# Hi and lo parts of six stationary operands, laid side by side element by element

## The chip, the cores and the metric

One core of one Trainium2 chip runs the kernel. The metric is the device time of one execution in microseconds (us), as the median of several runs.

## What is computed

The input `x` is (8, 1024, 256): 8 batches, 1024 tokens, 256 channels. Each token is normalised (layer norm without weights) to `xn`. Two blocks read `xn`, and the output is `x` plus both:

```python
# attention: 8 heads of 128, one shared key/value head, causal
q = xn @ Wq + bq                 # (T, 8, 128), plus positions
k, v = split(xn @ Wkv + bkv)     # (T, 128) each, k plus positions
out = softmax(mask(q @ k.T / sqrt(128))) @ v @ Wo
# channel mix
xr = mu_r * xn + (1 - mu_r) * xn_prev      # xn_prev: the token before
xk = mu_k * xn + (1 - mu_k) * xn_prev
ffn = sigmoid(xr @ W_r.T) * (relu(xk @ W_k.T) ** 2 @ W_v.T)
```

All is float32.

## The kernel before

**High and low parts.** TensorE is fed with tiles of type `float32r` (`R` in the code), which keep fewer bits than float32. So every operand is kept as two tiles: index 0 the rounded value (a copy on ScalarE), index 1 what is left (a subtraction on VectorE or GpSimd). A product then takes three passes of matmuls into the same accumulator: high by high, high by low, low by high (`PASSES`; `product` at L1036 does this for all but two kinds of work). `matmul(out, a, m)` loads `a`, 128 columns, into the array (an LDWEIGHTS, engine PEld in the profile) and streams `m` past it. Here `a` is called the standing or stationary operand, `m` the moving one. Each matmul has its own load.

**Order of work.** A batch has 1024 tokens in 8 tiles of 128 and 4 chunks of 256. A step `s` (64 per batch) takes 16 queries of all 8 heads, which makes 128 rows, against the keys up to them. The scores of a step have 16 to 1024 columns; from tile 4 on they are made in two halves. The steps are pipelined by fixed lags: scores (L1036, `pS<-kt,qt`), mask and minimum on VectorE, exponential on ScalarE, scaling on GpSimd, then the turn of the probabilities, for 40 of the 64 steps by TensorE (L1139) and for 24 by VectorE and a round trip through DRAM, and last the product with `v` (L1173, `pO<-pt,v`). Between these stand fillers, in an order written out by hand in `TURNS` and `WO_AT`:

- `Q`, four per chunk, 12 matmuls of 256 columns each: standing `wq`, moving `xt`.
- `KV`, one per chunk, 12 matmuls: standing `wkv`, moving `xt`.
- `FK`, 12 matmuls: standing `wk`, moving `mh`.
- `FR`, 12 matmuls: standing `mh`, moving `wr`.
- `FV`, 12 matmuls: standing `kh`, moving `wv`.
- `WO`, one per tile of 128 tokens, 24 matmuls (L1123): standing `ot`, moving `wo`.

In the scores `qt` stands and `kt` moves. In the product with `v`, `v` stands and `pt` moves; where the block on the diagonal is packed, one matmul with `vs` (L1181) takes the place of its three.

**Who writes the six operands of the change.** The weights are written once, at the start (`weight_hi`, `weight_lo`). `qt`: ScalarE at L661, GpSimd at L527. `ot`: ScalarE at L759, VectorE at L994. `kh`: ScalarE at L705, GpSimd at L590. The last three are written in each batch, in chunks or pairs of steps; `qt` and `ot` are scattered in runs of 16 elements already.

**Where the tiles lie.** `sb(...)` gives each tile the next free bytes of every partition, in the order of the code. All sizes down to `kh` and `ot` are multiples of 1024 bytes, so only `gap` shifts what comes after it: `xt`, `mh`, `wv`, `kt`, `pt`, `wo` start at a multiple of 1024, and `wq` to `ot` 64 bytes past one.

Of the kernel before, what the change touches and what calls it, by code (L numbers as in the profile page):

```python
# [4 lines left out]
B, T, E = 8, 1024, 256  # L5
H, D = 8, 128
P = 128
CT = E // P
CHUNK = 256
# [4 lines left out]
SUB = P // H  # L14
# [204 lines left out]
def build(nc, x_d, wq_d, wkv_d, wo_d, wr_d, wk_d, wv_d, bq_d, bkv_d, mu_d, pet_d, out_d, park_d):  # L219
    F, R = mybir.dt.float32, mybir.dt.float32r  # L220
# [5 lines left out]
    with ExitStack() as ctx:  # L226
        def sb(name, shape, dt=F):
            return ctx.enter_context(nc.sbuf_tensor(name, shape, dt))
# [11 lines left out]
        kt = [sb(f"kt{i}", [P, T], R) for i in range(2)]  # L240
        pt = [sb(f"pt{i}", [P, 2, NT, 2 * P], R) for i in range(2)]
        wo = [sb(f"wo{i}", [P, H, E], R) for i in range(2)]
        gap = sb("gap", [P, 16])
        wq = [sb(f"wq{i}", [P, CT, H * D], R) for i in range(2)]
        wk = [sb(f"wk{i}", [P, CT, E], R) for i in range(2)]
        wkv = [sb(f"wkv{i}", [P, CT, 2 * D], R) for i in range(2)]
        wr = [sb(f"wr{i}", [P, CT, E], R) for i in range(2)]
        kh = [sb(f"kh{i}", [P, CT, CHUNK], R) for i in range(2)]
        qt = [sb(f"qt{i}", [P, 2, CHUNK // SUB, H, SUB], R) for i in range(2)]
        v = [sb(f"v{i}", [P, NT, D], R) for i in range(2)]  # L250
        vs = sb("vs", [P, TPC, D], R)
        ot = [sb(f"ot{i}", [P, H, P], R) for i in range(2)]
        bq = sb("bq", [P, H])
        mu = sb("mu", [P, 4])
        omu = sb("omu", [P, 4])
# [1021 lines left out]
```

## Time and profile before

| | |
|---|---|
| median of 3 runs | 1517.11 us (1516.37 to 1522.73) |
| span of the profiled execution, first to last instruction | 1512.0 us |
| span of that execution beside the median | 5.1 us less |
| PE busy | 1484.7 us, 98% |
| DVE busy | 1262.6 us, 84% |
| POOL busy | 1153.7 us, 76% |
| ACT busy | 1052.6 us, 70% |
| matmuls, and as many weight loads | 11724 |

Busy time of PE is the union of its matmuls; a matmul's record runs from its start until its last column has left the array, so two that follow each other overlap. To see how fast the stream is, take the duration of a group of equal matmuls, subtract one matmul's duration and divide by their number less one: that is the distance from start to start. DVE is VectorE, ACT is ScalarE, POOL is GpSimd, SP is the engine that issues DMAs.

### The profile page before, as it was taken

Reading aid. Unit: us, or ns where it says so; the run is one execution under the profiler, and the core shown is the slowest. Engines: PE = TensorE matmul, PEld = TensorE weight load, DVE = VectorE, ACT = ScalarE, POOL = GpSimd, SP = SyncE. Lnnn points to the kernel's source line nnn. Section 1 sums busy time; section 2 is a strip of 40 time slices with the busy share of each in tenths; the row PEclk is TensorE's granted clock in tenths of the full one; section 3 lists DMA queues with packets and bytes.
Section 4 is the critical chain, followed back from the end, with each engine's and each line's share of the span. In section 5 each row is a group of like instructions: output and inputs, shape, how many; then the busy total and the mean of one; then the engine's idle time right before and its main releaser. Section 6 shows DMA issues by size and latency. Waiting matters only on the chain.

```text
span 1512.0 us, 36188 instructions
## 1 busy us (share of the span) xinstructions
PE 1484.7 (98%) x11724; PEld 1448.2 (96%) x11724; DVE 1262.6 (84%) x3424; ACT 1052.6 (70%) x2531; POOL 1153.7 (76%) x1665
## 2 busy tenths in 40 slices
PE   7999999999999999999999999999999999999998
PEld 6999999999999999999999999999999999999998
DVE  7988869888698896988879888788887988879875
ACT  5777667776677766767677676767767776777764
POOL 6787777787777787877778777778777787778774
PEclk9999999999999999999999999999999999999999
DMA  4144422444224542344423444134441344413453
GB/s 129 44 126 135 132 87 67 116 141 141 74 69 119 146 137 60 86 120 139 128 58 96 120 137 136 43 100 122 137 139 38 105 130 138 138 29 101 127 153 105
DMA packets 225801, 164.39 MB, mean 109 GB/s; under 512 B 51792, under 2 KB 220880, under 8 KB 225616
## 3 DMA queue, kind: packets, MB, share of 16 engines
q1 hardware_dynamic: 224768, 161.69, 37.1%
q8 instruction: 96, 1.57, 0.4%
q14 instruction: 89, 0.73, 0.2%
q10 hardware_dynamic: 848, 0.40, 0.1%
HBM read 81.27 MB, written 77.59 MB: 105 GB/s over the span
## 4 chain that ended last, share of the span: by engine, by line
PE 75%; DVE 10%; DMA 7%; SPq 3%; issue 3%; ACT 1%; POOL 1%; DVEq 0%; ACTq 0%; POOLq 0%
PE pS L1036 26%; PE pO L1173 21%; PE pG L1036 12%; PE pG L1123 8%; PE pT L1139 7%; DMA park_dram<-Y 5%; SPq L455 3%; DVE X L1015 2%; DVE mix L861 1%; DMA Z<-park_dram 1%; DVE Y L924 1%; DVE pt L940 1%; DVE qtmp L850 1%; PE pS L1123 1%; DVE xn L810 1%
## 5 line engine op out<-in xcount | busy, mean ns | idle before, releaser
L766 ACT ACTIVATE X<-X,bias 128x16 f32<-128x16 f32 (+56 forms) x512 | 376.0, 734 | 156.3 <-DVE bias L1015 154.8
L1036 PE MATMUL pS<-kt,qt 128*128 128x288 f32 (+41 forms) x2304 | 462.2, 329 | 4.1 <-DVE kv L837 2.5
L1173 PE MATMUL pO<-pt,v 128*128 128x256 f32 x3288 | 435.4, 283 | 2.5 <-DVE ot L994 2.4
L1173 PEld LDWEIGHTS pO<-pt,v 128*128 128x128 f32 x3288 | 399.8, 189 | 3.6 <-DVE ot L994 3.4
L575 POOL TENSOR_SCALAR X<-X,rec 128x16 f32<-128x16 f32 (+56 forms) x512 | 373.6, 730 | 26.9 <-DVE rec L914 16.2
L1015 DVE CUSTOM_DVE_ANT_0 X<-pS,mask 128x16 f32<-128x16 f32 (+56 forms) x512 | 353.7, 691 | 40.8 <-PE pS L1036 33.9
L1036 PEld LDWEIGHTS pS<-kt,qt 128*128 128x128 f32 x2304 | 365.2, 189 | 16.8 <-issue 3.7
L542 POOL TENSOR_TENSOR pt<-Z,pt 128x256 fp32r<-128x256 f32 (+5 forms) x192 | 317.7, 1655 | 78.7 <-ACT pt L688 77.8
L527 POOL TENSOR_TENSOR qt<-qtmp,qt 128x256 fp32r<-128x256 f32 x252 | 194.5, 772 | 62.8 <-ACT qt L661 55.2
L940 DVE TENSOR_TENSOR pt<-pT,pt 128x512 fp32r<-128x512 f32 (+3 forms) x440 | 207.7, 493 | 37.9 <-ACT pt L695 37.1
L759 ACT CAST ot<-pO 128x256 fp32r<-128x256 f32 x256 | 95.9, 375 | 173.4 <-PE pO L1173 94.3
L695 ACT CAST pt<-pT 128x512 fp32r<-128x512 f32 (+3 forms) x448 | 189.6, 453 | 11.8 <-PE pT L1139 11.4
L1139 PE MATMUL pT<-ident,X 128*128 128x128 f32 x1248 | 190.1, 274 | 0.8 <-DVE pt L940 0.8
L924 DVE STREAM_TRANSPOSE Y<-X 128x384 f32<-128x384 f32 (+5 forms) x192 | 172.1, 896 | 6.2 <-POOL X L575 3.8
L994 DVE TENSOR_TENSOR ot<-pO,ot 128x256 fp32r<-128x256 f32 x256 | 106.6, 416 | 83.6 <-ACT ot L759 82.1
L1123 PE MATMUL pG<-wo,ot 128*128 128x256 f32 x1344 | 169.7, 282 | 1.3 <-DVE qtmp L850 0.7
L688 ACT CAST pt<-Z 128x384 fp32r<-128x384 f32 (+5 forms) x192 | 148.1, 771 | 31.1 <-DMA Z<-park_dram 30.0
L1123 PEld LDWEIGHTS pG<-wo,ot 128*128 128x128 f32 x1344 | 160.0, 189 | 3.0 <-DVE qtmp L850 2.3
L1139 PEld LDWEIGHTS pT<-ident,X 128*128 128x128 f32 x1248 | 150.6, 141 | 9.9 <-POOL X L575 0.7
L1036 PE MATMUL pG<-xt,wq 128*128 128x256 f32 x1116 | 148.8, 283 | 1.3 <-POOL xt L515 0.8
L1036 PEld LDWEIGHTS pG<-xt,wq 128*128 128x128 f32 x1116 | 141.6, 190 | 4.5 <-DVE xtok L975 2.3
L573 POOL MEMSET X<- 128x16 f32 (+5 forms) x336 | 48.0, 143 | 105.1 <-DVE rec L914 104.5
(118 smaller groups left out, 1943.4 us busy)
## 6 DMA issues: line engine op xcount, KB each, us to landing
park_dram<-Y SPq DMA_DIRECT2D x32, 512.0 KB, 2.6
Z<-park_dram SPq DMA_DIRECT2D x128, 128.0 KB, 3.0
park_dram<-Y SPq DMA_DIRECT2D x32, 448.0 KB, 3.2
Z<-park_dram SPq DMA_DIRECT2D x128, 112.0 KB, 2.7
park_dram<-Y SPq DMA_DIRECT2D x32, 384.0 KB, 2.9
Z<-park_dram SPq DMA_DIRECT2D x128, 96.0 KB, 2.5
park_dram<-Y SPq DMA_DIRECT2D x32, 320.0 KB, 2.9
Z<-park_dram SPq DMA_DIRECT2D x128, 80.0 KB, 2.2
```

What stands on the lines that cost most here:

```text
L527: nc.gpsimd.tensor_tensor(qt[1][:, slot, :, h, :], qtmp[:, p % QTMP, i, :].rearrange("p (t q) -> p t q", q=SUB), qt[0][:, slot, :, h, :].b ...
L542: nc.gpsimd.tensor_tensor(pt_of(1, s)[:, 0:whole, :].rearrange("p k (a c) -> p a k c", a=4), Z[:, k % 2, :, 0:whole, :], pt_of(0, s)[:, 0: ...
L575: nc.gpsimd.tensor_scalar(x_row(s, 0, w), x_row(s, 0, w), rec[:, j:j + 1], 1.0, ALU.mult, ALU.mult).then_inc(normed, 1)
L695: nc.scalar.copy(pt_of(0, s)[:, k:k + nk, :], pT[u % 2][:, 0:nk * P].rearrange("p (k n) -> p k n", n=P)).then_inc(t_hi, 1)
L766: nc.scalar.activation(x_row(s, 0, w), x_row(s, 0, w), ACT.Exp, bias=bias[:, j:j + 1], scale=-1.0, accum_out=total[:, j:j + 1]).then_inc(e ...
L924: nc.vector.transpose(Y[:, k % 2, :, 0:nk, :].rearrange("p a k c -> p k a c"), x_row(s, 0, nk * P).rearrange("p (k a c) -> p k a c", a=4, ...
L940: low = nc.vector.tensor_tensor(pt_of(1, s)[:, k:k + whole, :], pT[u % 2][:, 0:whole * P].rearrange("p (k n) -> p k n", n=P), pt_of(0, s)[ ...
L1015: nc.vector.tensor_tensor_reduce(out=o, in0=scores, in1=m, scale=SCALE, scalar=HUGE, op0=ALU.add, op1=ALU.min, accum_out=bias[:, j:j + 1]) ...
L1036: last = nc.tensor.matmul(out, a[i], m[j], start=start and k == 0, stop=stop and k == n - 1)
L1123: last = nc.tensor.matmul(out[:, 0:E], ot[i][:, h, :], wo[j][:, h, :], start=(i, j, h) == (0, 0, 0), stop=i == 1 and h == H - 1)
L1139: last = nc.tensor.transpose(pT[u % 2][:, i * P:(i + 1) * P], x_row(s, (k + i) * P, (k + i + 1) * P), ident[:, :])
L1173: last = nc.tensor.matmul(pO[:, 0:2 * P], v[i][:, k, :], pt[j][:, pair % 2, k, :], start=n == 0, stop=n == 3 * nk - 1)
```

## The change

The pairs of tiles for `wq`, `wk`, `wkv`, `kh`, `qt` and `ot` become one tile each with a last dimension of 2: element 0 is the high part, element 1 the low one. Views with the old names index that dimension, so that the code that reads and writes them is as before, now with a step of 8 bytes from element to element in place of 4. The tiles also change order: `wqs`, `qts` and `ots` come right after `wo`; a gap of 32 bytes stands ahead of `wks`, another ahead of `wkvs`, a third ahead of `khs`. `wr`, `v` and `vs` come after two of the gaps.

```diff
-        gap = sb("gap", [P, 16])
-        wq = [sb(f"wq{i}", [P, CT, H * D], R) for i in range(2)]
-        wk = [sb(f"wk{i}", [P, CT, E], R) for i in range(2)]
-        wkv = [sb(f"wkv{i}", [P, CT, 2 * D], R) for i in range(2)]
+        wqs = sb("wqs", [P, CT, H * D, 2], R)
+        qts = sb("qts", [P, 2, CHUNK // SUB, H, SUB, 2], R)
+        ots = sb("ots", [P, H, P, 2], R)
+        gap0 = sb("gap0", [P, 8])
+        wks = sb("wks", [P, CT, E, 2], R)
+        gap1 = sb("gap1", [P, 8])
+        wkvs = sb("wkvs", [P, CT, 2 * D, 2], R)
         wr = [sb(f"wr{i}", [P, CT, E], R) for i in range(2)]
-        kh = [sb(f"kh{i}", [P, CT, CHUNK], R) for i in range(2)]
-        qt = [sb(f"qt{i}", [P, 2, CHUNK // SUB, H, SUB], R) for i in range(2)]
         v = [sb(f"v{i}", [P, NT, D], R) for i in range(2)]
         vs = sb("vs", [P, TPC, D], R)
-        ot = [sb(f"ot{i}", [P, H, P], R) for i in range(2)]
+        gap2 = sb("gap2", [P, 8])
+        khs = sb("khs", [P, CT, CHUNK, 2], R)
+        wq, wk, wkv, kh = [[w[:, :, :, i] for i in range(2)] for w in (wqs, wks, wkvs, khs)]
+        qt = [qts[:, :, :, :, :, i] for i in range(2)]
+        ot = [ots[:, :, :, i] for i in range(2)]
```

## Rows read from the trace of the kernel before

**Rows 1.** The page, busy us (share) xinstructions, and granted clock in 40 slices:
```profile
PE 1484.7 (98%) x11724; PEld 1448.2 (96%) x11724; DVE 1262.6 (84%) x3424; ACT 1052.6 (70%) x2531; POOL 1153.7 (76%) x1665
...
PEclk9999999999999999999999999999999999999999
```

**Rows 2.** The page, chain that ended last, by engine:
```profile
PE 75%; DVE 10%; DMA 7%; SPq 3%; issue 3%; ACT 1%; POOL 1%; DVEq 0%; ACTq 0%; POOLq 0%
```

**Rows 3.** Waits of PE, the longest: us in total, times, longest us:
```profile
PE pG L1081 <- DVE xtok L975: 4.1, 8, 0.6
```

**Rows 4.** Busy time of each engine in two stretches of a batch's length:
```profile
core 0: us, PE busy (x) PEld busy (x) DVE busy (x) ACT busy (x) POOL busy (x), PEclk, DMA share, GB/s
100.00:285.00 185.00, 184.07 (x1464) 179.90 (x1463) 155.94 (x426) 130.39 (x316) 143.72 (x208) 1.00 0.39 109
285.00:470.00 185.00, 183.93 (x1460) 179.72 (x1459) 155.81 (x426) 130.02 (x314) 143.03 (x206) 1.00 0.37 107
```

**Rows 5.** Order of time, PE: start us, us, instructions (x so many):
```profile
65.30 0.70 PE L1036 MATMUL pS<-kt,qt 128*128 128x400 f32 x3
...
193.96 1.56 PE L1036 MATMUL pS<-kt,qt 128*128 128x512 f32 x6
...
204.71 0.93 PE L1139 MATMUL pT<-ident,X 128*128 128x128 f32 x7
...
564.25 1.56 PE L1036 MATMUL pS<-kt,qt 128*128 128x512 f32 x6
...
593.71 1.66 PE L1036 MATMUL pS<-wr,mh 128*128 128x256 f32 x12
595.20 1.53 PE L1036 MATMUL pG<-xt,wq 128*128 128x256 f32 x12
...
622.17 2.98 PE L1123 MATMUL pS<-wo,ot 128*128 128x256 f32 x24
...
651.88 0.96 PE L1036 MATMUL pS<-kt,qt 128*128 128x288 f32 x6
...
667.33 3.09 PE L1123 MATMUL pG<-wo,ot 128*128 128x256 f32 x24 [0.26 <-DVE qtmp L850]
...
672.87 1.64 PE L1036 MATMUL pG<-xt,wq 128*128 128x256 f32 x12
```

**Rows 6.** Weight loads: three beside scores of 224 columns, and a mean:
```profile
601.22 0.41 PEld L1036 LDWEIGHTS pS<-kt,qt 128*128 128x128 f32 x3
...
L1036 PEld LDWEIGHTS pS<-kt,qt 128*128 128x128 f32 x2304 | 365.2, 189 | 16.8 <-issue 3.7 <-DVE kt L832 1.5 <-DVE bias L1015 0.6
```

**Rows 7.** Matmuls by form: busy us, mean ns of one:
```profile
L1139 PE MATMUL pT<-ident,X 128*128 128x128 f32 x1248 | 190.1, 274 | 0.8 <-DVE pt L940 0.8
L1123 PE MATMUL pG<-wo,ot 128*128 128x256 f32 x1344 | 169.7, 282 | 1.3 <-DVE qtmp L850 0.7 <-ACT ot L759 0.6
L1036 PE MATMUL pG<-xt,wq 128*128 128x256 f32 x1116 | 148.8, 283 | 1.3 <-POOL xt L515 0.8
...
L1036 PE MATMUL pS<-kt,qt 128*128 128x512 f32 x72 | 19.4, 395 | 0.0
L1036 PE MATMUL pS<-kt,qt 128*128 128x400 f32 x72 | 15.6, 343 | 0.0
L1036 PE MATMUL pS<-kt,qt 128*128 128x288 f32 x72 | 12.2, 295 | 0.0
```

**Rows 8.** Writers on ACT, POOL, DVE by form: busy us, mean ns of one:
```profile
L661 ACT CAST qt<-qtmp 128x512 fp32r<-128x512 f32 x128 | 79.8, 623 | 7.6 <-DVE qtmp L850 7.5
L679 ACT CAST mh<-mix 128x512 fp32r<-128x512 f32 x64 | 39.9, 624 | 24.8 <-DVE mix L861 18.4 <-PE pS L1036 6.3
...
L527 POOL TENSOR_TENSOR qt<-qtmp,qt 128x256 fp32r<-128x256 f32 x252 | 194.5, 772 | 62.8 <-ACT qt L661 55.2 <-DVE rec L914 7.4
L521 POOL TENSOR_TENSOR v<-kv,v 128x256 fp32r<-128x256 f32 x32 | 23.9, 746 | 5.3 <-ACT v L657 5.0
...
L994 DVE TENSOR_TENSOR ot<-pO,ot 128x256 fp32r<-128x256 f32 x256 | 106.6, 416 | 83.6 <-ACT ot L759 82.1
L975 DVE TENSOR_TENSOR xtok<-pG,xtok 128x256 f32<-128x256 f32 x56 | 23.2, 415 | 4.9 <-PE pG L1123 4.4
```

## Prediction

> **What bounds the kernel now.** I read the page's busy shares first, then the chain, TensorE's waits, and last its instructions in order of time. TensorE is busy for 98% of the span at full granted clock, which is the 2.4 GHz level [rows 1]. The chain that ended last is on PE for 75% [rows 2], and what PE waits for longest comes to 4.1 us in all, over 8 waits [rows 3]. Two stretches of 185 us, one batch each, show the same busy time within 0.2 us, with DVE at 84% and POOL at 77% [rows 4]. The kernel is a stream of 11,724 pairs of weight load and matmul, and its time is set by how far apart two matmuls start.
>
> That distance is the number to look at. A group of x matmuls of duration d lasts (x - 1) starts and one d. Means of one: 282 to 283 ns at 256 columns, 295 at 288, 343 at 400, 395 at 512, 274 for a transpose [rows 7]. With them the groups in order of time [rows 5] give:
> - seven transposes, whose standing operand is plain float32: (0.93 - 0.274)/6 = 109.3 ns;
> - twelve of `Q`: (1.53 - 0.283)/11 = 113.4 ns in one place, (1.64 - 0.283)/11 = 123.4 in another, the same code (the second holds a pause of some 80 ns before its second matmul, as the 24 of `WO` also do; without it 117 to 118);
> - 24 of `WO`: with such a pause of 85 ns taken off, (2.98 - 0.282 - 0.085)/23 = 113.6 on bank pS and (3.09 - 0.282 - 0.085)/23 = 118.4 on pG;
> - twelve of `FR` (standing `mh`, moving `wr`): (1.66 - 0.287)/11 = 124.8, again with a pause; 117 to 118 without;
> - scores: (1.56 - 0.395)/5 = 233.0 at 512 columns, (0.70 - 0.343)/2 = 178.5 at 400, (0.96 - 0.295)/5 = 133.0 at 288.
> At one column per tick of 2.4 GHz, 256 columns are 106.7 ns, 288 are 120.0, 400 are 166.7 and 512 are 213.3; the transposes' 109.3 lies 2.6 above 106.7. Against columns/2.4 + 2.6 ns the others are late by: 4 or 9 ns at 256 columns (two levels, nothing between them), 10.4 at 288, 9.2 at 400, 17.1 at 512. This lateness is no noise of other engines: six matmuls of 512 columns last 1.56 us in batch 2 and again in batch 4, and sit 370.29 us apart, two batches to 0.1 us [rows 5]. It belongs to TensorE's own two reading streams, the moving one and the weight loads beside it.
>
> **What the change does to those streams.** The number of instructions, their order, shapes and waits stay. Six standing operands (`wq`, `wk`, `wkv`, `qt`, `kh`, `ot`) get a step of 8 bytes in place of 4, and start at 0, 32, 64 or 96 bytes past a multiple of 1024, where all of them started at 64. `v`, `vs`, `wr` stay at 64 (two gaps of 32 bytes ahead of them), `mh` and the moving operands ahead of the gaps at 0. A load takes 128 elements; loads beside narrow score matmuls follow each other in (0.41 - 0.189)/2 = 110.5 ns [rows 6], about the time in which the moving stream takes 256. So before, the load walks 512 bytes while the moving stream walks 1024: it is overtaken, and each time they meet in one memory one may lose a slot. After, both walk 1024 bytes in the same time. Their distance stands still, and if they once meet, the one that loses a slot is then out of step and meets no more. That is my reason for a gain.
>
> Term 1, 256 columns: `WO` 64 tiles x 24 = 1536, `Q` 32 chunks x 48 = 1536, `KV`, `FK`, `FV` 384 each: 4224 matmuls. They sit at 113.5 or 118.3, about evenly: 116. They cannot go under the loads' own 110.5, nor under 109.3. I take 112, near the lower bound since that is the nearest row: 4 ns x 4224 = 16.9 us. Bounds: 109.3 gives 6.7 x 4224 = 28.3 us; no change gives 0; the unknown other side is in the rivals.
>
> Term 2, scores of over 256 columns: 384 in one piece (tiles 2 and 3) and 1536 in two (tiles 4 to 7): 1920. Mean lateness of the three widths above, (10.4 + 9.2 + 17.1)/3 = 12 ns. I leave 3 of it: 9 x 1920 = 17.3 us. Bounds: 0 and 12 x 1920 = 23.0. Narrower scores are paced by the loads and gain nothing.
>
> Term 3: 3288 of `pO<-pt,v` and 384 of `FR` keep operands, step and place: 0. They are what a run of after can be held against.
>
> Term 4, writers. ACT, DVE and POOL now write (and POOL and DVE read back) in steps of 8 bytes. No row shows a step of 8, so bounds by the nearest: the copy to `qt` scatters runs of 64 bytes and takes 623 ns, the contiguous one to `mh` 624; POOL's subtraction into `qt` 772 against 746 into contiguous `v`; DVE's into `ot`, in such runs too, 416 against 415 for a plain addition [rows 8]. I take 0; the bound is twice the POOL difference, 52 ns x 284 operations = 15 us of POOL, which works beside TensorE with 42 us free per batch [rows 4], and something like 30 ns on each of 256 `ot` copies and subtractions. These lie on the way to `WO`, but one group of `pO` work stands between; without that cover it would be 256 x 60 ns = 15 us.
>
> Sum: 16.9 + 17.3 = 34.2 us of TensorE. Not all arrives. A quarter of the chain is not PE [rows 2], and with PE faster by 2.3% DVE goes from 84% to 86% and the short waits grow. I keep 80%: 27 us. The span of 1512.0 becomes 1485. The runs' median of 1517.1 lies 5.1 above the span, so the time is 1490.
>
> One rule of the Trainium skill speaks against all of this. The rows show lateness of 4 to 17 ns in TensorE's streams [rows 5]. "TensorE: Matmul & The Clock Gate" (Step-by-step: what each phase is for) says that loading the next weights takes no read bandwidth from the running matmul, and "SBUF — State Buffer" (Who interferes with whom) that TensorE waits for no one. By it the lateness would be TensorE's own and terms 1 and 2 nothing: 1517.
>
> A second one bears on the step: "SBUF — State Buffer" (Specifications) has lines of 16 bytes and full bandwidth for at least two hits on each. A step of 8 bytes gives just two, so by it a load stays at its speed; no row here shows it.
>
> **Rivals.**
> A, nothing moves: the 4 and 9 ns are inside the fp32r matmul or the load's handover. For: all kinds of matmul show them, whatever tiles they read. Against: the same code sits at either of two levels, and transposes at 109.3 show none. Then only writers count: 1517, 1511 to 1523.
>
> B, slower: the streams now stay in step on the wrong distance, and a stall that used to come when one overtook the other comes all along. Place: every pair with a standing operand of the six. Price: the rows have one step of 4.8 ns between levels. All at the upper level: 2.3 x 4224 = 9.7 us, and 3 x 1920 = 5.8 for scores, so 15 us: 1533. One step above it: 7 x 4224 + 5 x 1920 = 39 us: 1556. It decides as soon as the mean start distance passes 116. For: a load now touches twice as many lines, and `wq`, `qt` and `ot` start at offset 0 like what moves beside them. Against: a lost slot puts them apart.
>
> C, the step halves the load's speed: a load takes twice 106.7 ns and sets the pace at some 217: 101 x 4224 = 427 us and about 100 more at the scores: over 2000. For: no row shows a strided load. Against: the moving stream already takes an element every 0.42 ns, so the memory gives 4 bytes at twice the load's rate.
>
> **How the numbers follow.** Forecast (1490, its own range 1466 to 1508): 0.55. A: 0.19. B: 0.21. C: 0.05. The lowest is both upper bounds kept whole, 1517 - 51 = 1466. The range goes from 1468 to 1538, over A and the milder half of B, and leaves out about 0.18. A difference under 0.5% (7.6 us) can't be told from none. Faster takes most of the forecast and a little of A: 0.57; same 0.18; slower 0.25.
>
> **What would show it.** Right: groups of twelve and 24 with `wq`, `ot`, `kh` at 109 to 112 ns per start, the 512-column scores near 218 and 1.5 us or less for six, while `pO<-pt,v` and `FR` stay at 113 and 118; mean load still 188 to 189 ns; batches of some 181.5 us. Term 1 is wrong if `WO` is still at 113 or 118; term 2 if six scores of 512 still take 1.56 us; term 4 if the copies to `qt` or `ot` are over 30 ns longer. If the batches shrink by much less than PE's starts, the 80% was too high. A load longer than 189 ns shows C, levels of 123 or more show B.

## The result, and the profile after

The kernel after takes 1528.44 us (median of 4 runs, 1528.09 to 1531.52), the one before 1516.74 beside it. The ratio is 1.008 (95% interval 1.0057 to 1.0104): 0.8% slower, where I had forecast 1.8% faster.

The page of after, busy time and chain:

```profile
span 1526.4 us, 36188 instructions
...
PE 1497.8 (98%) x11724; PEld 1468.6 (96%) x11724; DVE 1267.0 (83%) x3424; ACT 1067.4 (70%) x2531; POOL 1155.9 (76%) x1665
...
PE 88%; DVE 7%; issue 2%; DMA 1%; SPq 1%; ACT 0%; POOL 0%; DVEq 0%; ACTq 0%; POOLq 0%
```

PE is busy 13.1 us longer, of the 14.4 us by which the span has grown, and still 98% of the span. The kernel is bound as before; the stream of matmuls itself has become slower. Order of time, PE of after, the rows that answer to [rows 5]:

```profile
194.32 1.57 PE L1041 MATMUL pS<-kt,qts 128*128 128x512 f32 x6
...
569.41 1.57 PE L1041 MATMUL pS<-kt,qts 128*128 128x512 f32 x6
...
628.18 3.12 PE L1128 MATMUL pS<-wo,ots 128*128 128x256 f32 x24
...
664.99 1.60 PE L1041 MATMUL pG<-xt,wqs 128*128 128x256 f32 x12
...
669.26 1.54 PE L1178 MATMUL pO<-pt,v 128*128 128x256 f32 x12
```

With one matmul of mean duration taken off as in the prediction, `Q` starts every (1.60 - 0.286)/11 = 119.5 ns, against 113.4 where it ran well before; `WO` on bank pS goes from 2.98 us to 3.12, or from 113.6 to 119.5 ns (the pause of 85 ns taken off). Six scores of 512 columns last 1.57 us in place of 1.56. `pO`, which keeps its layout, has (1.54 - 0.282)/11 = 114. Weight loads of after by form, and three beside narrow scores (start us, us), the answer to [rows 6]:

```profile
L1178 PEld LDWEIGHTS pO<-pt,v 128*128 128x128 f32 x3288 | 396.8, 188 | 2.6 <-DVE ots L999 2.3
L1041 PEld LDWEIGHTS pS<-kt,qts 128*128 128x128 f32 x2304 | 374.7, 196 | 21.2 <-DVE kt L837 10.4 <-issue 1.6 <-DVE bias L1020 0.5
```
```profile
602.76 0.43 PEld L1041 LDWEIGHTS pS<-kt,qts 128*128 128x128 f32 x3
```

A load of the new layout takes 196 ns against 189, and its pace is (0.43 - 0.196)/2 = 117 ns against 110.5. The load of `v`, not changed, takes 188. The matmuls by form (busy us, mean ns), beside [rows 7]:

```profile
L1178 PE MATMUL pO<-pt,v 128*128 128x256 f32 x3288 | 431.9, 282 | 1.4 <-DVE ots L999 1.2
L1128 PE MATMUL pG<-wo,ots 128*128 128x256 f32 x1344 | 175.1, 286 | 0.8 <-ACT ots L764 0.6 <-DVE qtmp L855 0.2
L1041 PE MATMUL pG<-xt,wqs 128*128 128x256 f32 x1116 | 151.8, 286 | 1.5 <-POOL xt L520 1.5
```

The starts sum up to the whole difference. For each kind of matmul I added the distances from its starts to the start of whatever matmul comes next, pauses included, over the one profiled execution of each kernel, in us (`pO` with `vs`; the kernels of the last five rows are those of the experiments):

```
kernel           WO     Q    KV    FK    FV    FR     pO  scores  transposes   all
before        183.5 186.1  46.7  52.2  45.8  47.9  403.2   398.5       142.4  1506.5
after         189.6 191.0  48.3  59.5  47.6  47.6  398.8   397.1       141.3  1520.8
place alone   188.8 189.5  46.9  54.4  46.8  47.9  401.6   395.7       142.2  1513.7
step alone    190.4 191.8  48.3  56.5  47.6  47.6  400.3   400.6       142.3  1525.4
qt alone      184.8 187.0  46.6  52.0  46.3  47.9  401.2   401.1       142.2  1509.1
all but qt    190.0 192.4  48.3  56.1  47.6  47.9  402.0   395.6       142.3  1522.2
no gap        189.2 190.2  47.7  58.7  47.1  48.5  416.6   395.6       140.8  1534.4
```

`WO`, `Q`, `KV` and `FV` are 14.4 us longer and `FK` 7.3; `pO` and the scores give 5.8 back and the rest 1.4, which leaves the 14.3 but for rounding. The distances inside groups have changed from a mix of 113 and 118 to an even 120.

Some 6 of the 7.3 us of `FK` are no slower stream but a wait: once in each batch, behind `FK` and ahead of scores of 264 columns, TensorE waits for VectorE's copy of `kv`. The waits of PE, before and then after (us in total, times, longest us):

```profile
PE pS L1036 <- DVE kv L837: 2.5, 7, 1.3
```
```profile
PE pS L1041 <- DVE kv L842: 9.3, 8, 1.3
```

It doesn't need the writing in steps: it is 9.0 us in the kernel without a gap below too, where every tile is contiguous. Why it grows with a slower stream no run shows.

### The profile page after: what moved, and what is told of

Same layout as the page of the kernel before. It is cut to its first block, busy times and chain, and to the rows that moved or that the text cites. A ratio compares the mean times of both kernels' runs of the same rounds, so it can differ in the third digit from the quotient of the medians.

```text
span 1526.4 us, 36188 instructions
## 1 busy us (share of the span) xinstructions
PE 1497.8 (98%) x11724; PEld 1468.6 (96%) x11724; DVE 1267.0 (83%) x3424; ACT 1067.4 (70%) x2531; POOL 1155.9 (76%) x1665
## 4 chain that ended last, share of the span: by engine, by line
PE 88%; DVE 7%; issue 2%; DMA 1%; SPq 1%; ACT 0%; POOL 0%; DVEq 0%; ACTq 0%; POOLq 0%
PE pS L1041 31%; PE pO L1178 23%; PE pG L1041 14%; PE pG L1128 9%; PE pT L1144 8%; PE pS L1128 2%; DVE mix L866 1%; DVE X L1020 1%; DVE Y L929 1%; DVE pt L945 1%; DVE xn L815 1%; PE pG L1086 1%; PE pS L1086 0%; DMA park_dram<-Y 0%; DVE gate L971 0%
## 5 line engine op out<-in xcount | busy, mean ns | idle before, releaser
L1041 PE MATMUL pS<-kt,qts 128*128 128x288 f32 (+41 forms) x2304 | 466.3, 331 | 10.7 <-DVE kv L842 9.3
L1178 PE MATMUL pO<-pt,v 128*128 128x256 f32 x3288 | 431.9, 282 | 1.4 <-DVE ots L999 1.2
L1041 PEld LDWEIGHTS pS<-kt,qts 128*128 128x128 f32 x2304 | 374.7, 196 | 21.2 <-DVE kt L837 10.4
L532 POOL TENSOR_TENSOR qts<-qtmp,qts 128x256 fp32r<-128x256 f32 x252 | 196.3, 779 | 71.6 <-ACT qts L666 70.3
L764 ACT CAST ots<-pO 128x256 fp32r<-128x256 f32 x256 | 101.9, 398 | 187.6 <-PE pO L1178 99.7
L999 DVE TENSOR_TENSOR ots<-pO,ots 128x256 fp32r<-128x256 f32 x256 | 107.0, 418 | 90.0 <-ACT ots L764 87.8
L1128 PE MATMUL pG<-wo,ots 128*128 128x256 f32 x1344 | 175.1, 286 | 0.8 <-ACT ots L764 0.6
L1128 PEld LDWEIGHTS pG<-wo,ots 128*128 128x128 f32 x1344 | 165.4, 196 | 2.4 <-DVE qtmp L855 1.4
L1041 PE MATMUL pG<-xt,wqs 128*128 128x256 f32 x1116 | 151.8, 286 | 1.5 <-POOL xt L520 1.5
L1041 PEld LDWEIGHTS pG<-xt,wqs 128*128 128x128 f32 x1116 | 145.1, 197 | 3.3 <-issue 1.5
```

What stands on the lines that cost most here:

```text
L532: nc.gpsimd.tensor_tensor(qt[1][:, slot, :, h, :], qtmp[:, p % QTMP, i, :].rearrange("p (t q) -> p t q", q=SUB), qt[0][:, slot, :, h, :].b ...
L1041: last = nc.tensor.matmul(out, a[i], m[j], start=start and k == 0, stop=stop and k == n - 1)
L1128: last = nc.tensor.matmul(out[:, 0:E], ot[i][:, h, :], wo[j][:, h, :], start=(i, j, h) == (0, 0, 0), stop=i == 1 and h == H - 1)
L1178: last = nc.tensor.matmul(pO[:, 0:2 * P], v[i][:, k, :], pt[j][:, pair % 2, k, :], start=n == 0, stop=n == 3 * nk - 1)
```

## The experiments

Theory S: a strided load is slower by itself. Rival P: where the tiles start is what costs. Each ratio is against the kernel before as it ran beside that experiment; its medians there were 1514.7 to 1517.0 us.

**TensorE alone.** Groups of 24 matmuls on data of `x`, in `WO`'s pass order, with a chosen step and start, both counted in elements of 4 bytes (`...` stands for what is left out):

```diff
+        def standing(step, off, i, h):
+            if step == 1:
+                a = off + i * 1024 + h * P
+            else:
+                a = off + i + h * P * step
+            return S[:, a:a + P * step] if step == 1 else S[:, a:a + (P - 1) * step + 1:step]
...
+                for i, j, h in order: last = mm(ps[:, 0:64], standing(2, 16, i, h), M[:, j, h, 0:64], ...)  # step 8 B, offset 64 B, 64 columns
+                n += 1; last.then_inc(done, 1); pe.wait_ge(done, n)
```

> A kernel of TensorE groups alone: x goes in and comes out unchanged, none of the reference's arithmetic is done. 39 groups of 24 matmuls in the pass order of WO, each on its own line, run three times, while the other engines rest. They differ in the standing operand's step (4, 8, 12, 16, 32 bytes), its start (0 to 128 bytes past the moving one's) and the moving columns (64, 256, 512). Theory S (a strided load is itself slower): at 64 columns, where the loads set the pace, starts are 111 ns apart at 4 bytes and 117 to 118 at 8 bytes, and more at 12 or above; the same at every offset; at 256 columns 113 or 118 at step 4 and 120 at step 8. Rival P (the place decides): at 64 columns steps 4 and 8 agree within 2 ns, and at 256 columns the distance changes by 4 ns or more with the offset. If other engines' traffic caused the lateness, all groups sit at 109 to 110 at 256 columns here.

Measured: no other compute engine works, and still 256 columns at step 4 have a median of 120 ns per start at offset 0 and of 117 to 119 at 16 to 128. So the lateness is TensorE's own. At 256 columns and full clock, steps of 8, 12, 16 and 32 bytes give medians of 120, 173, 235 and 244 ns. In the groups of 64 columns the granted clock fell to 0.5 within the second one (step 8), and it stayed there into the first group of 256 columns, which read (5.27 - 0.415)/23 = 211 ns per start, about 256 columns at 1.2 GHz; these groups are set aside, and the second probe repeats them. The groups of 512 columns depend on the start of the load as well: their median is 227 ns with it at 0 or 16 and 235 at 64.

```profile
103.37 5.87 PE L80 MATMUL ps<-M,S 128*128 128x512 f32 x24
...
171.85 5.74 PE L114 MATMUL ps<-M,S 128*128 128x512 f32 x24
```

L80 has its load at 64 and L114 at 0, both at step 4; each holds one pause of about 110 ns.

**The place alone.**

```diff
-        gap = sb("gap", [P, 16])
         wq = [sb(f"wq{i}", [P, CT, H * D], R) for i in range(2)]
+        qt = [sb(f"qt{i}", [P, 2, CHUNK // SUB, H, SUB], R) for i in range(2)]
+        ot = [sb(f"ot{i}", [P, H, P], R) for i in range(2)]
+        gap0 = sb("gap0", [P, 8])
         wk = [sb(f"wk{i}", [P, CT, E], R) for i in range(2)]
+        gap1 = sb("gap1", [P, 8])
         wkv = [sb(f"wkv{i}", [P, CT, 2 * D], R) for i in range(2)]
...
+        gap2 = sb("gap2", [P, 8])
+        kh = [sb(f"kh{i}", [P, CT, CHUNK], R) for i in range(2)]
```

> The order of tiles and the three gaps of after, but high and low parts in two tiles each, step 4 bytes: placement alone. Theory S: as before within 0.3%, 1512 to 1522 us, narrow scores paced at 111 to 112 ns. Rival P (start at 0, 32 or 96 bytes is what costs): 1526 to 1531 us, like after, with WO at 120 ns.

1522.39 us, ratio 1.0049 (1.0035 to 1.0063). Neither was met: it is about half of the loss. At a start of 0 `WO` and `Q` go to 119.6 and 119.2 ns with contiguous loads; `wkv`, left at 64, stays at 115.2; narrow scores keep their distances. Place matters to the contiguous layout.

**The step alone.**

```diff
-        gap = sb("gap", [P, 16])
-        wq = [sb(f"wq{i}", [P, CT, H * D], R) for i in range(2)]
+        gap0 = sb("gap0", [P, 16])
+        wqs = sb("wqs", [P, CT, H * D, 2], R)
+        wq = [wqs[:, :, :, i] for i in range(2)]
...                                 # wk, wkv, kh, qt and ot alike, each in its old place
```

> The order of tiles and the one 64-byte gap of before, but the six operands side by side: the step alone. Theory S: 1525 to 1532 us, WO at 120 ns per start, narrow scores paced at 117 to 118. Rival P: 1512 to 1520 us.

1530.68 us, ratio 1.010 (1.0081 to 1.0118), as S said; `WO` 120.1, `Q` 120.2. Rival P falls as a cause of the change's loss: with the old places the side-by-side layout is as slow as with the new ones. Step and place don't add up (0.5% and 1.0% against 0.8% together).

**The operand of the scores alone, and all but it.**

> Before, with qt alone side by side (the scores). Theory S: only the 384 narrow scores are paced by loads (6 ns each, 2 us), the 1920 wide ones hide the load, so 1516 to 1521 us, and 1.56 to 1.60 us for six scores of 512. Rival P: no change within 0.2%. If the loads' longer reading disturbs the moving stream in proportion, wide scores lose 3 ns or more each and it is 1522 or more.

1517.48 us, ratio 1.0015 (1.000 to 1.003). Wide scores changed by 1 ns each (mean lateness over columns/2.4, inside groups: 16.2 against 15.0), narrow ones pace at 117. The load is all but hidden behind wide scores.

> Before's order of tiles and gap, with wq, wk, wkv, kh and ot side by side and qt left in two tiles: the counterpart of e3_qt. The 4224 matmuls of 256 columns go from 116 to 120 ns per start, 17 us, less what the wide scores and pO give or take by themselves: 1526 to 1531 us, most of e2_step's 1530.7. If the scores carried the cost, within 4 us of before.

1527.7 us, ratio 1.0067 (1.0049 to 1.0084). Five operands of 256-column work carry the loss. An estimate from the distances is 4 ns x 4224 = 17 us; in the table their five kinds are 20.1 us longer, pauses and the wait for `kv` included, and scores and `pO` 4.1 shorter; the time grew by 12.

**What paces a load and what paces the moving stream.** The second kernel of TensorE alone varies both steps; a step of 0 reads one element again and again.

> A second kernel of TensorE groups alone (x goes in and comes out, the reference's arithmetic is left out), each group of 24 now behind 24 matmuls of 512 columns so that the clock stays at full. Theory L (each stream reads SBUF in lines of 16 bytes and gets one in some 1.83 ns): loads alone (64 columns moving) 111 to 112 ns at steps 0 and 4 bytes, 117 at 8, 173 at 12, 234 at 16; 256 columns moved with step 0 fall to 109 to 112 when the load has step 0 or 4 as well; moved with step 8 they take 2 x 117 = 234 whatever the load does; 512 columns with step 0 take 216 and with step 4 226 to 236. Rival M (the two streams disturb each other): with the load's step 0, 256 columns at step 4 fall to 109 to 111, and with the moving step 0 a load of step 8 falls to 111. The start of the standing operand, 0 to 256 bytes in steps of 16: theory L alone gives no change; if placement matters as the run e1_place says (119.6 for WO at 0, 115.8 at 64), the groups at 64 are 2 to 4 ns below those at 0 and the pattern repeats with some power of two.

Order of time in it (start us, us; one line of code per group):

```profile
61.17 3.03 PE L68 MATMUL ps<-M,S 128*128 128x256 f32 x24
...
96.23 2.89 PE L80 MATMUL ps<-M,S 128*128 128x256 f32 x24
...
218.85 3.04 PE L122 MATMUL ps<-M,S 128*128 128x256 f32 x24
...
236.48 2.84 PE L128 MATMUL ps<-M,S 128*128 128x256 f32 x24
245.08 2.89 PE L131 MATMUL ps<-M,S 128*128 128x256 f32 x24
...
265.26 2.84 PE L137 MATMUL ps<-M,S 128*128 128x256 f32 x24
273.87 5.67 PE L140 MATMUL ps<-M,S 128*128 128x256 f32 x24
285.30 2.98 PE L143 MATMUL ps<-M,S 128*128 128x256 f32 x24
...
305.48 4.26 PE L149 MATMUL ps<-M,S 128*128 128x256 f32 x24
...
337.07 5.64 PE L158 MATMUL ps<-M,S 128*128 128x256 f32 x24
...
426.28 5.34 PE L182 MATMUL ps<-M,S 128*128 128x512 f32 x24
437.38 5.71 PE L185 MATMUL ps<-M,S 128*128 128x512 f32 x24
...
459.96 5.76 PE L191 MATMUL ps<-M,S 128*128 128x512 f32 x24
482.59 5.76 PE L197 MATMUL ps<-M,S 128*128 128x512 f32 x24
```

The lines are, with the mean distance of starts ("at" is the start in bytes):

```
line   standing        moving   columns   ns per start
L128   step 0          step 0   256       111.5
L137   step 4 at 64    step 0   256       111.5
L143   step 8          step 0   256       117.3
L149   step 12         step 0   256       170.7  (median 173)
L158   step 16         step 0   256       227.9  (median 233)
L131   step 0          step 4   256       113.5
L140   step 4 at 64    step 8   256       228.7
L80    step 4 at 64    step 4   256       113.8
L68    step 4 at 0     step 4   256       119.7
L122   step 8 at 64    step 4   256       120.0
L182   step 0          step 0   512       215.7
L185   step 0          step 4   512       231.2
L191   step 4          step 4   512       233.2
L197   step 8          step 4   512       233.3
```

Three facts come out. First, with the moving step at 0 the load is alone, and it costs by the 16-byte pieces it touches: 64 of them at 8 bytes 117.3 ns, 96 at 12 bytes 173, 128 at 16 bytes 233, or 1.80 to 1.83 ns for each. Beyond 16 bytes little more is due: at 32 the first probe has 244 against 235. The groups of 64 columns, loads alone in another way, say the same: medians of 112, 112, 118, 173 and 233 ns at steps of 0, 4, 8, 12 and 16 bytes. At 4 bytes there are 32 pieces, and 111.5 ns are paced by the elements. Eight bytes is just over the point where the pieces take the lead. The Trainium skill ("SBUF — State Buffer", Specifications) has lines of 16 bytes and full bandwidth for two hits on each; the lines agree, the full bandwidth does not: two hits cost a load 5%.

Second, the moving stream pays a like price for itself. With the load at step 0, 512 columns (128 pieces) take 231.2 at step 4 and 215.7 at step 0; 256 columns take 113.5 and 111.5, and 229 at step 8, twice as much. So most of the lateness of scores of 512 columns is their own reading; for the other widths, 10 ns late, no run takes the streams apart. It isn't a fixed amount: the first probe has 227 with a dense load at 0. No load tried brought 512 dense columns under that, so 11 ns over 215.7 stay with the moving stream, and up to 8 hang on where the load starts. In the kernels this doesn't show: scores of 512 columns are 233.0 ns apart before and 232.8 without a gap, with `qt` at 0. For 256 dense columns the lowest in any probe is 113 to 114, not 109.3.

Third, something remains between the streams. At step 4 it makes 113.8 to 120 according to the start: 113.8 at 64 and from 116.7 to 120.0 at the other 16 starts tried. At step 8 it is 119.7 at 0, 120.0 at 64 and 121.3 at 112, where the load alone has 117.3: of the 120 ns of the change, 117.3 are the load's own pace, which no start tried got under, and 2 to 3 ns come on top from the two streams together. What makes these no run shows. Rival M, in which the step of one stream sets the other's speed, falls for the load: with the moving stream at step 0 the load of step 8 keeps its 117.3.

**No gap.**

```diff
- gap = sb("gap", [P, 16])
```

> Before without its 64-byte gap: all standing operands, wr and v too, start at a multiple of 1024 as the moving ones do, step 4 bytes. From e1_place, where WO and Q went from 116 to 119.4 ns per start at offset 0: 3.5 x (4224 + 3288 of pO) = 26 us, some 1538 to 1545 us. Rival (the offset works only through the order of tiles): within 3 us of before.

1539.63 us, ratio 1.0145 (1.012 to 1.0169), 22.7 us slower. By form:

```profile
L1172 PE MATMUL pO<-pt,v 128*128 128x256 f32 x3288 | 448.9, 287 | 1.9 <-DVE ot L993 1.7
L1122 PE MATMUL pG<-wo,ot 128*128 128x256 f32 x1344 | 174.4, 286 | 0.9 <-ACT ot L758 0.6 <-DVE qtmp L849 0.3
```

`WO` at 174.4 us is where after has it (175.1); `pO`, which after leaves at 64, goes from the 435.4 of before to 448.9 (431.9 in after). The distance of 64 bytes between standing and moving operand is worth 4 ns per matmul of 256 columns in the contiguous layout. The change gave it up for `wq`, `qt` and `ot` (0) and for `wk` and `kh` (32 and 96), and at step 8 there was nothing to keep: 64 is no better than 0.

**Twelve bytes in the kernel.** `wk` and the high part of `wkv` share a tile of three. (A first form, `wk` alone padded to a step of 12 bytes, did not fit in SBUF and has no time.)

```diff
- wk = [sb(f"wk{i}", [P, CT, E], R) for i in range(2)]
- wkv = [sb(f"wkv{i}", [P, CT, 2 * D], R) for i in range(2)]
+ wks = sb("wks", [P, CT, E, 3], R)
+ wkv1 = sb("wkv1", [P, CT, 2 * D], R)
+ wk = [wks[:, :, :, i] for i in range(2)]
+ wkv = [wks[:, :, :, 2], wkv1]
```

> Before with three tiles side by side at a step of 12 bytes: the two parts of wk and the high part of wkv; everything else as before. Theory L (16-byte lines, one in 1.83 ns): all 384 loads of FK and two thirds of the 384 of KV read 96 lines and set the pace at 173 ns: 640 x 56 = 36 us, 1550 to 1556 us. If what costs in the change is any step at all, at 4 ns a load as in after, 640 x 4 = 3 us and 1518 to 1522.

1543.32 us, ratio 1.017 (1.0136 to 1.0205). One group of `FK`:

```profile
619.15 2.34 PE L1038 MATMUL pS<-mh,wks 128*128 128x256 f32 x12
```

That is, with its pause of 85 ns and a duration of 344 off, (2.34 - 0.344 - 0.085)/11 = 174 ns per start. The starts give 172.4 for `FK` and 175.8 for the strided loads of `KV`. The price per line holds in the kernel. The time grew by 27 us and not by 36. The profiled execution was the longest of the four (1547.1 us): in it `FK` and `KV` are 38.0 us longer than before, scores 3.1 and `WO` 1.7 shorter (114.7 ns per start in place of 115.8), and the span grew by 33.

**Can 113 be had everywhere?** A third kernel of TensorE alone entered the groups behind matmuls of different widths.

> TensorE alone again (x goes in and comes out, the reference's arithmetic is left out), standing and moving step 4 bytes, 256 columns. 18 starts of the standing operand (0, 40 to 88 in steps of 4, 128, 320, 576, 1088 bytes), each with six matmuls of other widths (16 to 500 columns) ahead of the group, to enter it at another phase. If the distance of 64 bytes alone decides, every entry at 64 gives 113.8 ns per start and other distances 117 to 120. If the entry decides too, as the two levels of 113 and 118 in the kernel before suggest, the six entries at 64 split between 113.8 and 118. If there is a more robust start, all six of its entries are at 113 to 114; 320, 576 and 1088 tell with which period it repeats.

```profile
248.49 2.90 PE L211 MATMUL ps<-M,S 128*128 128x256 f32 x24
251.73 2.89 PE L214 MATMUL ps<-M,S 128*128 128x256 f32 x24
255.01 2.99 PE L217 MATMUL ps<-M,S 128*128 128x256 f32 x24
```

All three have the start at 64; they enter behind 264, 392 and 500 columns and run at 113.9, 113.7 and 117.8. Most groups keep one level to their end: these are the two levels of the kernel before. In the first of its passes starts of 64, 320, 576 and 1088 gave equal distances at all six entries, so the pattern repeats with 256 bytes; in the second pass 64 changed its level at three entries and 320 at one. A start of 76 had the lower level at all six entries, 52 and 88 at five. Three kernels put 76 or 88 in:

```diff
- gap = sb("gap", [P, 16])
+ gap = sb("gap", [P, 19])          # 76 bytes; 22 for 88
...
+ gap_end = sb("gap_end", [P, 13])  # behind ot; 10 for 88
```

> Before with its gap at 76 bytes in place of 64 (and 52 bytes behind the standing operands, so that what follows stands as before). In the third probe a start at 64 took 113.8 ns per start at four entries and 118 at two, a start at 76 took 113.3 to 114.5 at the three wide entries and the same as the lower level at the narrow ones. If that carries over to the kernel, WO, Q, KV, FV and pO go from 116 to about 114.3: 1.6 x 7100 = 11 us, 1504 to 1508 us. Rival: beside other engines' traffic the two levels stay about even, 1513 to 1519 us.

> The same with 88 bytes (and 40 behind). In the probe 114.3 to 116.7 at the wide entries: 1505 to 1511 us if it carries over, 1513 to 1519 if not.

> 76 bytes between standing and moving operand in all kinds of work: wr at a multiple of 1024 with the other moving ones, mh at 76, wk at 152. FR (117.6 before) and FK (117.6) go to 114.3 as well: 768 x 3.3 = 2.5 us under e9_gap76, 1502 to 1506 us. Rival: within 2 us of e9_gap76.

1527.31, 1527.03 and 1528.4 us, ratios 1.0078 (1.0055 to 1.0102), 1.0072 (1.005 to 1.0093) and 1.0089 (1.0066 to 1.0111). All three forecasts missed, in the other direction: at 76 the groups run in patterns of 116 to 120 ns, 117.7 on average for `WO`, and never settle at 113. The probe differs from the kernel in the rest of its layout, in the traffic beside it and in how groups are entered; which of these breaks the lower level I did not find. No version beat the kernel before.

## Why the prediction was wrong

The forecast was 1490 us, 1.8% faster; measured were 1528.4, inside the stated range of 1468 to 1538, but only because the range took in the milder half of rival B; the mechanism forecast had the other sign. What bounds the kernel, the count of 4224 and 1920 matmuls, and that the stream's start distances would decide the time, held. So did the level of all that was left alone (`FR` 117 to 118, `pO` 113 or 118), and the mark that it named for a slower load, over 189 ns, is what the rows of after show (196).

**The step that failed** is the reason for a gain: "each time they meet in one memory one may lose a slot. After, both walk 1024 bytes in the same time", and the lateness "belongs to TensorE's own two reading streams", taken as their disturbing each other. That it is TensorE's own is right. But a stepped load is slower by itself, 117.3 ns against 111.5, over the lower level and over the old mean of 116; the gain had no room. And much of the lateness is the moving stream's own pace, as the standing step of 0 shows: 2.0 of the 2.3 ns by which the lower level at 256 columns (113.8) lies over the loads' 111.5, and 15.5 of 17.5 at 512 with the load at 64 (11 by the first probe's lowest). Between the streams are the distance from the lower level to the upper one and the 2 to 3 ns at step 8. I had excluded other engines by the repetition of a row [rows 5], and took the only other stream as the culprit; a third answer, the stream itself, I gave only to rival A.

**Term 1** took 112 for the new distance, from the loads' own 110.5. It kept the old load pace for the new layout. Measured: 120, a loss of 4 ns in place of a gain of 4, on each of 4224 matmuls. I had a bound for strided writers, but none for the strided load other than rival C. The row that warned was [rows 6] itself: the loads' pace of 110.5 was already over what 256 columns need, 106.7, so that any price on the load would be paid at once.

**Term 2**: 17.3 us of gain forecast. The scores' starts sum to 397.1 against 398.5; inside groups the wide ones are 1.7 ns farther apart than before, not 9 closer (16.7 against 15.0 over columns/2.4). Neither a gain nor the cause of the loss was there.

**Term 3**: `FR` as said. `pO` took 4.4 us less, since more of its groups fell into the lower level. It was not forecast, and no run ties it to the change; the third probe shows that the entry to a group alone can decide.

**Term 4**: POOL 779 against 772 and DVE 418 against 416, as taken. ScalarE's copies did get longer, the one to `qt` by more than the 30 ns that the prediction named as the sign that term 4 is wrong:

```profile
L764 ACT CAST ots<-pO 128x256 fp32r<-128x256 f32 x256 | 101.9, 398 | 187.6 <-PE pO L1178 99.7 <-PE pO L1186 76.8 <-PE pG L1128 9.3
L666 ACT CAST qts<-qtmp 128x512 fp32r<-128x512 f32 x128 | 85.9, 671 | 7.5 <-DVE qtmp L855 7.3
```

`qt` 671 against 623 [rows 8] and `ot` 398 against 375. That is 48 x 128 + 23 x 256 = 12 us of an engine with 30% to spare. `WO` waits for what ScalarE writes in `ot` for 0.6 us in all, as before (0.6), so it cost nothing that can be seen.

**Readings that were off.** Two stretches agree within 0.2 us for PE and DVE only; ACT differs by 0.4 and POOL by 0.7 [rows 4], which changes nothing. The base of 109.3 ns is that of transposes, which move 128 columns of plain float32 and not 256 of float32r [rows 5]: it is no floor for the others, and that transposes show no lateness spoke less against rival A than I let it. The bound of 28.3 us in term 1 goes down to 109.3, under the loads' own 110.5 that the same sentence calls a limit; with 110.5 it is 23.2. The 178.5 ns at 400 columns come from one group of three; over all groups inside the kernel it is 181.0.

**The rivals.** The outcome, 1528, lies just under the milder end of B (1533), and by its mark, a mean over 116 per start, B is what happened; levels of 123 or more, its other mark, did not come. Its mechanism, streams in step on a wrong distance, is not shown: at step 8 starts of 0 and 64 give the same, and a load alone is already slow. C was right in kind, a slower load, and off in size: half speed comes at a step of 16 bytes, not 8. The rule of the Trainium skill that I set against the change ("TensorE: Matmul & The Clock Gate", Step-by-step: what each phase is for), that a load takes nothing from the running matmul, fits the part of the lateness that stays with the load at step 0; against it stand 3 to 6 ns at 256 columns and up to 8 at 512 that depend on where the load starts (113.8 against 119.7, 227 against 235).

## What to carry to other kernels

Where each matmul has its own weight load, compare the two paces before touching either: here 111.5 ns for a load and 113.5 for 256 columns, so that 5% on the load costs at once, and the same 5% is nearly free beside scores of 264 to 512 columns (1 ns per matmul with `qt` alone). Keep what TensorE reads dense: here it paid 1.8 ns per line of 16 bytes touched. A step of 8 bytes, two elements per line, cost a load 5% (117.3 against 111.5) and doubled the time of a moving operand (229 against 113.8). To find out whether two streams disturb each other, let one of them read a single element again and again, and see whether the other gets faster.

## What the runs showed of the hardware that was not expected

- TensorE's moving read is slower than a column per tick even when every byte is used: 512 dense float32r columns took 231 ns (227 at the best start of the load), as many columns from one element 215.7. The 231 fit lines of 16 bytes at the loads' price (128 lines, 1.81 ns each); 256 dense columns, 64 lines, took 113.5, a little less than that.
- The start of the standing operand against the moving one, modulo 256 bytes, is worth 3 to 6 ns per 256 columns, and most groups keep the level they were entered with: 113.7 or 117.8 with the same addresses.
- The granted clock fell to 0.5 around stretches of 64 columns per load, although TensorE's pauses there were no longer than 0.2 us: in the first probe from 59.2 to 83.1 us, behind groups of 64 columns from 54.3 us on; in the second from 374.9 to 378.3 us, just behind a group of 24 such matmuls (371.5 to 374.3 us, loads 112 ns apart), but not behind the same group in its second pass (804.4 us). It was 1.0 throughout the third probe (span 966.2 us).
